# Attention probabilities turned and multiplied one step later, in a kernel of sixteen pipelined sequences

## The chip, the cores and the metric

The kernel runs on one core of a Trainium2 chip. The metric is device time in microseconds (us) from the first to the last instruction of one execution, with what lies around it. Five engines each work through a queue of their own in order: PE multiplies matrices, DVE, ACT and POOL work elementwise, SP issues DMAs. They meet only through semaphores, so an instruction that waits holds up all that stands behind it on its engine. PE writes to PSUM; DVE and ACT read PSUM, POOL doesn't.

## The reference

Sixteen sequences of 256 tokens and 128 features go through two layers. The first is a small two-layer network whose weights are trained while it runs: for each of its steps it computes an output with weights that the gradient of that step has just updated, so each step needs the one before it.

```
grads = grad(loss)(params, z, y)
new_params = params - LR * grads
out = recon(new_params, x @ t_q.T)        # scan over steps
```

The second is attention with 16 heads of 64 over 4 groups of keys and values, causal, with a window of 128 tokens and a learned sink in each head's denominator, and then a mixture of 32 experts of which each token uses 4.

```
q, k, v = split(rmsnorm(x) @ qkv_w + qkv_b);  q, k = rope(q), rope(k)
logits = where(mask, -inf, q k^T / 8)
attn = exp(logits - logaddexp(logsumexp(logits), sink))
x = x + (attn @ v) @ proj_w + proj_b
x = x + sum over the top 4 experts of gate * (silu(h2 Wg) * (h2 Wu)) @ Wd
```

## The kernel before, in words

The program has a short preparation, a part `layers` (from the start to about 940 us of the profile) and a part `experts`. The change is in `layers`, which is one loop of iterations n = 0 to 19. Iteration n holds five sequences at once, each at another stage: sequence n in the trained network (call it F), n-1 in the output with the new weights and its normalisation (O), n-2 in the projection to queries, keys and values and their rotation (N), n-3 in attention (A), n-4 in the output projection, the choice of experts and their slots (B). POOL sends the rows of sequence n-5 to the experts' table by indirect DMAs (line 94).

Each iteration has six steps, u = 0 to 5. Attention of a sequence is cut into six units of two head groups (h = 0, 1); units 0, 1, 3, 4 have two head pairs and queries 128 to 255, which see two blocks of keys; units 2 and 5 have four pairs and queries 0 to 127, one block. The order of the work within a step is written out for each engine in its function `iteration`, with tables `side` that place the stages of the other sequences; there is no planner. In step u of the kernel before:

- PE: projection of chunk u (line 555), scores of unit u+1 (lines 373, 379), probabilities times values of unit u-1 (line 408), stages of other sequences, turning of unit u's probabilities for h = 0 (line 393), more stages, turning of the rotated queries or keys (line 566), turning of unit u for h = 1.
- DVE: `quotients` for h = 0 of unit u (adds the sink term, line 672, reciprocal, 674, scales the probabilities in place, 678 or 682), the rotation's products (826 to 830), stages, `maxima` of unit u+1 (694 to 700), `quotients` for h = 1, stages.
- ACT: the sink's exponential (1008), exponentials of unit u for h = 0 (1020), copy of the turned probabilities of unit u-1 for h = 1 out of PSUM (1030), exponentials for h = 1, stages, copy of the product y of unit u-1 (1039), copy of the turned probabilities of unit u for h = 0, stages, copy of the turned queries or keys (`qk_out`).
- POOL: sum of the rotation's products (1152), then two sends of rows, then small stages: `rms2` in step 2, `norms` (1160 to 1174) in step 4, `spread` in step 5.

There is one buffer `prob` for each h: the exponentials of the next unit wait until this unit's has been turned. There are three banks of scores for two heads, so scores of unit u+1 wait until the exponentials of unit u, h = 0, have read theirs (line 370). The values `vv` have two buffers.

The chain through the trained weights runs over a whole iteration: `x_turn` (421) and `z_products` in step 0, `a_products` and `z_rows` in step 1, `gelus` on ACT (1063, another function table than Exp) and `residual_cols` (468, 470) in step 2, `residual_rows` (479 to 482), DVE's `slope_cdf` (759 to 765) and `hidden_grad` in step 3, `output` (PE 505, DVE 781 to 787) in step 4, and in step 5 `gradients` (517 to 523), DVE's `update` of the weights (803 to 808) and `norm_turn` (537). `norm_turn` waits for `update` and for `normed_rows` (795), which waits for POOL's `norms`, which wait for `output`. After `norm_turn` ACT's `hT_out` (1082) gives the next iteration's chunk 0 its input.

Of the kernel before, what the change touches and what calls it, by code (L numbers as in the profile page):

```python
# [24 lines left out]
P = 128  # L25
# [201 lines left out]
def layers(m):  # L227
# [12 lines left out]
    with ExitStack() as ctx:  # L240
# [27 lines left out]
        vv = sb("vv", [P, 2, TPS, KV * DH])  # L268
# [3 lines left out]
        sums, rec = (sb(n, [P, 2, 4]) for n in "sums rec".split())  # L272
        prob, probT = sb("prob", [P, 2, 512]), sb("probT", [P, 2, 512])
# [30 lines left out]
        def run(iteration):  # L304

            for n in range(SEQS + 4):
                iteration(n, n % 2)
# [45 lines left out]
        def _(pe):  # L353
# [29 lines left out]
            def turn_probs(n, par, u, h):  # L383
                A, ap, u, done = at_unit(n, par, u)
                if not live(A):
                    return
                if h == 0:
                    after(pe, s["probT"], 2 * done - 3)
                else:
                    after(pe, s["yT"], done - 1)  # L390
                pe.wait_ge(s["normed"], 2 * done - 1 + h)
                for k in range(4):
                    ins = tr(turned[h][:, k * P:(k + 1) * P], prob[:, h, k * P:(k + 1) * P], ident[:])  # L393
                ins.then_inc(s["t_ps"], 1)

            def values(n, par, u):
# [6 lines left out]
                for i in range(len(pairs)):  # L403
                    for k in range(2 if second else 1):
                        for h in range(2):
                            g = 2 * g2 + h
                            blk = 2 * i + k if second else i
                            ins = mm(turned[1][h * DH:(h + 1) * DH, i * P:(i + 1) * P], vv[:, ap, k, g * DH:(g + 1) * DH],  # L408
# [148 lines left out]

            def qk_turn(n, par, c):
# [11 lines left out]
            def project(t, k):  # L570

                def stage(n, par):
                    B = n - 4
                    if not live(B):
                        return
                    cols = slice(t * P, (t + 1) * P)
                    if t == 1 and k == 0:
                        after(pe, s["place"], B)

                    pe.wait_ge(s["yT"], B * UNITS + (2 if t else 3) + 3 * k)  # L580
                    if k == 0:
                        bias(side_g[:, cols], QKV, QKV + D)
                    for p in range(4 * k, 4 * k + 4):
                        ins = mm(side_g[:, cols], yT[:, par, p, cols], m["wproj"][:, p, :], start=False,
                                 stop=(p == PAIRS - 1))
                    ins.then_inc(s["proj_ps"], 1)
                return stage
# [21 lines left out]
            def ranks(n, par):  # L609
# [5 lines left out]
                for t in range(TPS):  # L615
# [6 lines left out]

            side = {0: [x_turn, project(1, 0)], 1: [z_products, project(1, 1)], 2: [a_products, project(0, 0)],
                    3: [z_rows, project(0, 1)], 5: [residual_cols], 6: [residual_rows, h2_turn],
                    7: [hidden_grad, gate], 8: [output], 10: [ranks, gradients], 11: [norm_turn]}

# [4 lines left out]

            def iteration(n, par):
                for u in range(UNITS):
                    if n != 2 or u == 0:
                        qkv(n, par, u)
                    if n == 2 and u < UNITS - 1:
                        qkv(n, par, u + 1)
# [5 lines left out]
                    if n < 3 or n == SEQS + 3:  # L643
                        keep_clock(1, turned[0] if n < 3 else score[2])
                    for stage in side.get(2 * u + 1, []):
                        stage(n, par)
                    qk_turn(n, par, u)
                    turn_probs(n, par, u, 1)
                    if n < 3 or n == SEQS + 3:
                        keep_clock(1, turned[0] if n < 3 else score[2])  # L650
# [6 lines left out]
            run(iteration)  # L657

        @block.vector
        def _(v):  # L660
            V = nc.vector

            def quotients(n, par, u, h):
# [5 lines left out]
                one = 2 * done - 1 + h  # L669
                v.wait_ge(s["es_out"], done)  # L670
                v.wait_ge(s["exped"], one)
                V.tensor_tensor(sums[:, h, 0:w], sums[:, h, 0:w], es[:, b, h, 0:w], ALU.add).then_inc(s["den"], 1)  # L672
                v.wait_ge(s["den"], one)
                V.reciprocal(rec[:, h, 0:w], sums[:, h, 0:w]).then_inc(s["rec"], 1)
                v.wait_ge(s["rec"], one)
                if second:
                    for j in range(w):
                        ins = V.tensor_scalar(prob[:, h, j * TOK:(j + 1) * TOK], prob[:, h, j * TOK:(j + 1) * TOK],  # L678
                                              rec[:, h, j:j + 1], None, ALU.mult)
                else:  # L680
                    rows = prob[:, h, :].rearrange("p (j k) -> p j k", j=w)
                    ins = V.tensor_tensor(rows, rows, rec[:, h, :][:, :, None].broadcast_to([P, w, P]), ALU.mult)
                ins.then_inc(s["normed"], 1)

            def maxima(n, par, u):
# [5 lines left out]
                sink = sink_s[:, pairs[0] // 2] if second else sink_f[:, pairs[0] // 4]  # L691
                v.wait_ge(s["s_ps"], done)
                for h in range(2):
                    V.tensor_reduce(mx[:, b, h, 0:w], score[(2 * u + h) % 3][:].rearrange("p (j k) -> p j k", j=w), AX.X,  # L694
                                    ALU.max).then_inc(s["mx"], 1)
                v.wait_ge(s["mx"], 2 * done)
                V.scalar_tensor_tensor(out=nm[:, b, :, 0:w], in0=mx[:, b, :, 0:w], scalar=-0.125, in1=sink,
                                       op0=ALU.mult, op1=ALU.min).then_inc(s["nm"], 1)
                v.wait_ge(s["nm"], done)
# [3 lines left out]
            def x_norm(n, par):  # L703

                F = n + 1
                if not live(F):
                    return
                if n in (0, 1):
                    v.wait_ge(s["rs0"], 2 * n + 4)
# [200 lines left out]
            def slots(n, par):  # L910
                B = n - 4
                if not live(B):
# [10 lines left out]
            side = {2: [a_bias], 3: [a_rows], 4: [attended], 5: [slope_pdf, h2_rows], 6: [slope_cdf],  # L923
                    7: [pick, hidden_grad], 8: [one_hot], 9: [output], 10: [normed_rows, places],
                    11: [x_norm, slots]}

            def first_stats(u):

# [7 lines left out]
            def iteration(n, par):  # L936
                for u in range(UNITS):
                    quotients(n, par, u, 0)
                    rope(n, par, u)
                    if n == 0:  # L940
                        first_stats(2 * u)
                    for stage in side.get(2 * u, []):
                        stage(n, par)
                    maxima(n, par, u + 1)
                    if u == 5:
                        update(n, par)
                    quotients(n, par, u, 1)
                    if u == 1:
                        centred(n, par)
                    if n == 0:  # L950
                        first_stats(2 * u + 1)
                    for stage in side.get(2 * u + 1, []):
                        stage(n, par)
# [40 lines left out]
            v.wait_ge(s["rs0"], 2)  # L994
            x_norm(-1, 1)
            run(iteration)

        @block.scalar
        def _(act):
# [10 lines left out]
            def exps(n, par, u, h):  # L1010
# [5 lines left out]
                after(act, s["t_ps"], 2 * done - 3 + h)  # L1016
# [610 lines left out]
```

## Time and profile before

| | us |
|---|---|
| three runs of the kernel | 1217.37, 1218.06, 1222.43 |
| their median | 1218.06 |
| the profiled execution's own time | 1224.69 |
| its span, first to last instruction | 1222.9 |
| granted PE clock, mean of the span, of full speed | 0.891 |

The profiled execution is a single one. Its span lies 1.8 us below its own time, and its time 6.6 us above the median of the runs. In the profile an engine's row says what it did and when; the time in brackets is idle time just before an instruction, with the work that released it. Several instructions of one line are merged into one row with their count. Full speed of PE's clock is 2.4 GHz; a granted clock of 0.50 is 1.2 GHz.

### The profile page before, as it was taken

The numbers are of one execution on the slowest core, as the hardware profiler recorded it, in microseconds if no ns is written. First come the engines' busy times: TensorE is split into PE (matmuls) and PEld (weight loads), VectorE is DVE, ScalarE is ACT, GpSimd is POOL, SyncE is SP. The second block draws the span as 40 slices with busy tenths as digits, with TensorE's granted clock in tenths as the row PEclk, the third lists the DMA queues.
The fourth block names the chain that finished last, engine by engine and source line by source line (L and its number), as shares of the span: only waits on it lengthen the run. The fifth ranks groups of instructions, "written<-read, shape, count | busy, mean of one in ns | idle before, by whom it ended". The sixth has DMA issues, their size and how long they took to land. (4 is left out here: it accounts for less than half of the span.)

```text
span 1222.9 us, 21965 instructions
## 1 busy us (share of the span) xinstructions
PE 951.9 (78%) x6783; PEld 702.7 (57%) x6865; DVE 778.4 (64%) x2648; ACT 608.3 (50%) x1987; POOL 495.6 (41%) x643
## 2 busy tenths in 40 slices
PE   4778888897989888898988988888877399777710
PEld 2445666565666666575666666555555288666610
DVE  4455687778677776868786777877764344333307
ACT  1017565655646565655756555665654155444400
POOL 2221223334334333334343333434432457777760
PEclk7788999899889899998989989998997599999855
DMA  5999999990000000000000000000000144443119
GB/s 142 267 356 376 374 376 371 370 300 10 16 6 18 9 15 11 11 10 11 15 8 18 6 15 11 11 15 11 15 15 15 55 115 134 132 115 104 52 54 338
DMA packets 98372, 131.54 MB, mean 108 GB/s; under 512 B 15025, under 2 KB 54866, under 8 KB 98258
## 3 DMA queue, kind: packets, MB, share of 16 engines
q1 hardware_dynamic: 84690, 108.36, 26.9%
q0 software_dynamic: 9216, 19.68, 4.6%
q10 hardware_dynamic: 4352, 2.10, 0.6%
q8 instruction: 57, 0.93, 0.3%
q14 instruction: 57, 0.47, 0.1%
HBM read 30.34 MB, written 99.75 MB: 106 GB/s over the span
## 5 line engine op out<-in xcount | busy, mean ns | idle before, releaser
L1152 POOL TENSOR_TENSOR l_t_cos<-l_t_cos,l_t_sin 128x512 f32<-128x512 f32 (+1 forms) x96 | 104.4, 1088 | 434.1 <-DVE l_t_sin L830 434.1
L1020 ACT ACTIVATE l_prob<-l_score,l_nm 128x128 f32<-128x128 f32 (+1 forms) x512 | 210.8, 431 | 0.0
L393 PE MATMUL l_turned<-ident_sb,l_prob 128*128 128x128 f32 x768 | 127.3, 291 | 90.2 <-DVE l_prob L678 52.4
L1345 POOL DMA_INDIRECT expert_out<-e_yo,e_dest x160 | 153.7, 960 | 69.1 <-issue 37.2
L1030 ACT COPY l_probT<-l_turned 128x512 f32<-128x512 f32 x192 | 113.0, 589 | 102.5 <-PE l_turned L393 101.5
L393 PEld LDWEIGHTS l_turned<-ident_sb,l_prob 128*128 128x128 f32 x768 | 91.4, 149 | 108.2 <-issue 107.3
L94 POOL DMA_INDIRECT expert_rows<-h,slot x128 | 128.9, 1007 | 37.6 <-issue 32.4
L694 DVE TENSOR_REDUCE l_mx<-l_score 128x2 f32<-128x512 f32 (+1 forms) x192 | 122.7, 680 | 10.6 <-PE l_score L379 10.2
L555 PE MATMUL l_side_q<-wqkv_sb,l_hT 128*128 128x512 f32 x186 | 118.5, 725 | 12.0 <-issue 4.1
L379 PE MATMUL l_score<-l_kT,l_qT 64*128 64x128 f32 (+1 forms) x1024 | 115.4, 356 | 0.0
L1020 ACT ACTIVATION_READ_ACCUMULATOR l_prob<-l_score,l_nm 128x1 f32 x512 | 110.7, 216 | 0.0
L379 PEld LDWEIGHTS l_score<-l_kT,l_qT 64*128 64x128 f32 x1024 | 79.0, 195 | 52.5 <-issue 48.9
L408 PE MATMUL l_turned<-l_probT,l_vv 128*64 128x128 f32 x1536 | 106.9, 282 | 1.4 <-ACT l_probT L1030 1.4
L408 PEld LDWEIGHTS l_turned<-l_probT,l_vv 128*64 128x64 f32 x1536 | 83.4, 138 | 27.4 <-issue 21.5
L1486 ACT ACTIVATE e_yo<-e_p_y,e_mine 128x128 f32<-128x128 f32 x160 | 45.8, 369 | 88.3 <-DMA expert_out<-e_yo,e_dest 77.3
L1039 ACT COPY l_yT<-l_turned 128x256 f32<-128x256 f32 (+1 forms) x96 | 42.2, 439 | 88.8 <-PE l_turned L408 88.8
L672 DVE TENSOR_TENSOR l_sums<-l_sums,l_es 128x2 f32<-128x2 f32 (+1 forms) x192 | 30.6, 159 | 86.1 <-ACT l_prob L1020 85.5
L678 DVE TENSOR_SCALAR l_prob<-l_prob,l_rec 128x256 f32<-128x256 f32 x256 | 79.8, 354 | 4.5
L1427 DVE COPY e_hidT<-e_p_h 128x512 f32<-128x512 f32 x40 | 27.7, 692 | 83.9 <-PE e_p_h L1553 78.0
L1543 PE MATMUL e_p_up<-wup_sb,e_xT 128*128 x320 | 79.7, 394 | 0.0
L1562 PE MATMUL e_p_y<-wdown_sb,e_hidT 128*128 x320 | 48.0, 297 | 29.6 <-ACT e_yo L1486 29.5
L826 DVE TENSOR_TENSOR l_t_cos<-l_side_q,rope_sb 128x512 f32<-128x512 f32 (+1 forms) x93 | 55.4, 596 | 24.4 <-PE l_side_q L555 24.1
(234 smaller groups left out, 1937.2 us busy)
## 6 DMA issues: line engine op xcount, KB each, us to landing
expert_rows<-zeros SPq DMA_DIRECT2D x32, 2240.0 KB, 21.9
e_xt<-expert_rows SPq DMA_DIRECT2D x160, 70.0 KB
e_rows<-expert_out SPq DMA_DIRECT2D x16, 512.0 KB, 5.9
wup_sb<-in_wup SPq DMA_DIRECT2D x1, 4096.0 KB, 14.5
expert_out<-e_yo,e_dest POOLq DMA_INDIRECT x160
expert_rows<-zeros SPq DMA_DIRECT2D x32, 70.0 KB, 2.1
expert_rows<-zeros SPq DMA_DIRECT2D x4, 560.0 KB, 12.9
expert_rows<-h,slot POOLq DMA_INDIRECT x128, 2.3
```

Source lines behind the costliest of these rows:

```text
L94: m["nc"].gpsimd.indirect_dma_start(m["xs"], bass.IndirectOffsetOnAxis(ap=m["slot"][:, par, c:c + 1], axis=0), m["h2"][:, par, c // TOPK, ...
L379: ins = mm(bank[h][:, i * w:(i + 1) * w], qT[rows, ap, p, tok], kT[rows, ap, g2, 0:w], start=False, stop=(i == len(pairs) - 1))
L393: ins = tr(turned[h][:, k * P:(k + 1) * P], prob[:, h, k * P:(k + 1) * P], ident[:])
L408: ins = mm(turned[1][h * DH:(h + 1) * DH, i * P:(i + 1) * P], vv[:, ap, k, g * DH:(g + 1) * DH], probT[:, h, blk * P:(blk + 1) * P], start ...
L555: mm(dst[:], hT[:, t * P:(t + 1) * P], m["wqkv"][:, part * 512:(part + 1) * 512], start=False, stop=True).then_inc(s["qkv_ps"], 1)
L678: ins = V.tensor_scalar(prob[:, h, j * TOK:(j + 1) * TOK], prob[:, h, j * TOK:(j + 1) * TOK], rec[:, h, j:j + 1], None, ALU.mult)
L694: V.tensor_reduce(mx[:, b, h, 0:w], score[(2 * u + h) % 3][:].rearrange("p (j k) -> p j k", j=w), AX.X, ALU.max).then_inc(s["mx"], 1)
L1020: ins = A_.activation(prob[:, h, cols], score[(2 * u + h) % 3][:, cols], ACT.Exp, bias=nm[:, b, h, j:j + 1], scale=0.125, accum_out=sums[: ...
L1030: A_.copy(probT[:, h, :], turned[h][:]).then_inc(s["probT"], 1)
L1152: g.tensor_tensor(t_cos[:, c % 2, 0:w], t_cos[:, c % 2, 0:w], t_sin[:, c % 2, 0:w], ALU.add).then_inc(s["added"], 1)
L1345: g_.indirect_dma_start(m["ys"], bass.IndirectOffsetOnAxis(ap=dest[:, g % FOUND, j:j + 1], axis=0), yo[:, g % YO, j, :], None).then_inc(se ...
L1543: ins = mm(p_up[g % 2][:, j, :], xT[:, g % 2, j, :], m["wup"][:, bass.ds(expert(g, j) * (2 * DFF), 2 * DFF)], start=True, stop=True)
```

## The change

Turning, copying and multiplying of unit u's probabilities move from step u (and the first part of step u+1) to step u+1. On PE the product with the values now ends the step, and the two turnings stand behind the scores. On ACT both heads' exponentials open the step, then come the sink's exponential, the copies of the turned probabilities of the unit before, and the copy of y ends the step. On DVE the sums and reciprocals of both heads of a unit are one operation each, placed behind the maxima of the next unit and interleaved with its shift and sink terms, and both scalings follow. `prob`, `sums` and `rec` get a second buffer by u % 2, `vv` a third. The loops over steps and the tables `side` are written out as lists of calls; DVE runs one iteration (n = -1) ahead for the first `x_norm`, and ACT and PE one iteration beyond, in which nothing is live. POOL's order and its DMAs are the same calls as before.

```diff
-        vv = sb("vv", [P, 2, TPS, KV * DH])
+        vv = sb("vv", [P, 3, TPS, KV * DH])
...
-        sums, rec = (sb(n, [P, 2, 4]) for n in "sums rec".split())
-        prob, probT = sb("prob", [P, 2, 512]), sb("probT", [P, 2, 512])
+        sums, rec = (sb(n, [P, 2, 2, 4]) for n in "sums rec".split())
+        prob, probT = sb("prob", [P, 2, 2, 512]), sb("probT", [P, 2, 512])
...
             def iteration(n, par):
-                for u in range(UNITS):
...
-                    scores(n, par, u + 1)
-                    values(n, par, u - 1)
-                    for stage in side.get(2 * u, []):
-                        stage(n, par)
-                    turn_probs(n, par, u, 0)
...
-                    qk_turn(n, par, u)
-                    turn_probs(n, par, u, 1)
...
+                chunk(n, par, 2)
+                scores(n, par, 3)
+                turn_probs(n, par, 1, 0)
+                turn_probs(n, par, 1, 1)
+                idle(n, par, 4)
+                residual_cols(n, par)
+                qk_turn(n, par, 2)
+                values(n, par, 1)
...
+                chunk(n, par, 5)
+                scores(n + 1, 1 - par, 0)
+                turn_probs(n, par, 4, 0)
+                ranks(n, par)
+                gradients(n, par)
+                turn_probs(n, par, 4, 1)
+                idle(n, par, 10)
+                norm_turn(n, par)
+                qk_turn(n, par, 5)
+                values(n, par, 4)
...
         @block.vector
...
-            def quotients(n, par, u, h):
+            def sums_out(n, par, u):
...
+                v.wait_ge(s["es_out"], done)
+                v.wait_ge(s["exped"], 2 * done)
+                V.tensor_tensor(sums[:, b, :, 0:w], sums[:, b, :, 0:w], es[:, b, :, 0:w], ALU.add).then_inc(s["den"], 1)
...
+                V.reciprocal(rec[:, b, :, 0:w], sums[:, b, :, 0:w]).then_inc(s["rec"], 1)
...
+                slope_cdf(n, par)
+                maxima(n, par, 4)
+                shifts(n, par, 4)
+                sums_out(n, par, 3)
+                sinks(n, par, 4)
+                recips(n, par, 3)
+                scaled(n, par, 3, 0)
+                scaled(n, par, 3, 1)
...
+                pick(n, par)
+                hidden_grad(n, par)
+                rope(n, par, 4)
...
+                scaled(n, par, 4, 1)
...
+                output(n, par)
+                rope(n, par, 5)
...
+                normed_rows(n, par)
+                places(n, par)
+                maxima(n + 1, 1 - par, 0)
+                shifts(n + 1, 1 - par, 0)
+                sums_out(n, par, 5)
+                sinks(n + 1, 1 - par, 0)
+                recips(n, par, 5)
+                update(n, par)
+                scaled(n, par, 5, 0)
...
         @block.scalar
...
-                after(act, s["t_ps"], 2 * done - 3 + h)
+                after(act, s["t_ps"], 2 * done - 5 + h)
...
-                    sink_terms(n, par, u)
-                    exps(n, par, u, 0)
-                    take_probs(n, par, u - 1, 1)
-                    exps(n, par, u, 1)
...
-                    take_y(n, par, u - 1)
-                    take_probs(n, par, u, 0)
...
-                    qk_out(n, par, u)
...
+                exps(n, par, 2, 0)
+                exps(n, par, 2, 1)
+                sink_terms(n, par, 2)
+                take_probs(n, par, 1, 0)
+                gelus(n, par)
+                take_probs(n, par, 1, 1)
+                rT_out(n, par)
+                qk_out(n, par, 2)
+                take_y(n, par, 1)
+                exps(n, par, 3, 0)
```

The lists of the other steps follow the same pattern; `chunk` is the projection with the exception for n = 2, `idle` the matmuls that fill PE in iterations 0 to 2 and 19.

## Rows read from the trace of the kernel before

**Rows 1.** Stretches (us, from:to, length): busy PE, PEld, DVE, ACT, POOL; clock; DMA.

```profile
142.70:798.00 655.30, 565.21 (x4319) 411.24 (x4379) 494.76 (x1688) 385.04 (x1307) 241.13 (x340) 0.93 0.23 81
...
581.30:634.10 52.80, 45.76 (x362) 33.34 (x366) 41.31 (x142) 31.94 (x110) 20.43 (x29) 0.97 0.04 12
...
848.90:899.20 50.30, 39.98 (x301) 26.53 (x304) 34.44 (x114) 27.71 (x101) 17.85 (x20) 0.90 0.04 13
...
899.20:938.40 39.20, 30.44 (x273) 23.00 (x274) 25.51 (x95) 23.54 (x89) 12.12 (x15) 0.87 0.05 18
```

**Rows 2.** Line 393 (probabilities turned): what PE waited for, us, times.

```profile
  DVE l_prob L678: 53.2, 44
  DVE l_prob L682: 37.8, 26
```

**Rows 3.** PE in order of time: start, us, instruction, idle before it and its releaser.

```profile
580.75 0.44 PE L537 MATMUL l_side_f<-ident_sb,l_hn 128*128 128x128 f32 x2
...
582.61 1.02 PE L555 MATMUL l_side_q<-wqkv_sb,l_hT 128*128 128x512 f32 x2
...
599.38 1.02 PE L555 MATMUL l_side_q<-wqkv_sb,l_hT 128*128 128x512 f32 x2
...
600.52 0.59 PE L373 MATMUL l_score<-mask,ident_bf 128*128 128x512 bf16 x2
...
602.11 1.09 PE L408 MATMUL l_turned<-l_probT,l_vv 128*64 128x128 f32 x16
...
607.37 0.63 PE L393 MATMUL l_turned<-ident_sb,l_prob 128*128 128x128 f32 x4 [1.98 <-DVE l_prob L682]
...
608.91 0.59 PE L373 MATMUL l_score<-mask,ident_bf 128*128 128x512 bf16 x2
...
616.62 0.63 PE L393 MATMUL l_turned<-ident_sb,l_prob 128*128 128x128 f32 x4 [1.40 <-DVE l_prob L678]
...
633.56 0.44 PE L537 MATMUL l_side_f<-ident_sb,l_hn 128*128 128x128 f32 x2 [1.15 <-DVE b_sb L808]
```

**Rows 4.** DVE and POOL in order of time, same iteration.

```profile
612.93 0.23 DVE L759 COPY l_h<-l_side_f 128x66 f32<-128x66 f32 x1 [1.57 <-PE l_side_f L482]
...
619.28 0.69 DVE L826 TENSOR_TENSOR l_t_cos<-l_side_q,rope_sb 128x512 f32<-128x512 f32 x1 [0.79 <-PE l_side_q L555]
...
626.44 0.25 DVE L787 BATCH_NORM_AGGREGATE l_mv<-l_stats 128x2 f32<-128x6 f32 x2
...
629.81 1.52 DVE L795 TENSOR_SCALAR l_hn<-x_all,l_mv,l_rms 128x128 f32<-128x128 f32 x2 [0.70 <-POOL l_rms L1174]
...
629.58 0.20 POOL L1174 TENSOR_TENSOR l_rms<-l_sq,l_rs 128x2 f32<-128x2 f32 x1
```

**Rows 5.** ACT in order of time, same iteration.

```profile
594.23 0.37 ACT L1039 COPY l_yT<-l_turned 128x256 f32<-128x256 f32 x1 [0.63 <-PE l_turned L408]
...
598.88 0.36 ACT L1020 ACTIVATE l_prob<-l_score,l_nm 128x128 f32<-128x128 f32 x1
...
602.28 1.28 ACT L1063 ACT_TABLE_LOAD   x1
...
603.58 0.63 ACT L1063 ACTIVATE l_hT<-l_aT 32x512 f32<-32x512 f32 x1
...
606.03 1.28 ACT L1008 ACT_TABLE_LOAD   x1
...
607.44 0.46 ACT L1020 ACTIVATE l_prob<-l_score,l_nm 128x256 f32<-128x256 f32 x1
```

**Rows 6.** DVE by line and shape: one or two heads' sums: busy us, mean ns.

```profile
L672 DVE TENSOR_TENSOR l_sums<-l_sums,l_es 128x2 f32<-128x2 f32 x128 | 20.1, 157 | 74.0 <-ACT l_prob L1020 73.4 <-ACT l_es L1008 0.3 <-issue 0.3
...
L672 DVE TENSOR_TENSOR l_sums<-l_sums,l_es 128x4 f32<-128x4 f32 x64 | 10.4, 163 | 12.1 <-ACT l_prob L1020 12.0
```

**Rows 7.** One-us stretches, columns as in rows 1.

```profile
607.20:608.20 1.00, 0.83 (x6) 0.82 (x7) 0.97 (x7) 0.99 (x5) 0.92 (x3) 1.00 0.20 72
618.20:619.20 1.00, 1.00 (x3) 0.28 (x2) 0.29 (x2) 1.00 (x8) 0.00 (x0) 0.50 0.02 8
```

More of the change, by code:

```diff
@@ L302, in live, with run @@
             return 0 <= k < SEQS
-        def run(iteration):
-            for n in range(SEQS + 4):
+        def run(iteration, early=0, late=0):
+            for n in range(-early, SEQS + 4 + late):
                 iteration(n, n % 2)
@@ L567, in qk_turn, with project @@
                 ins.then_inc(s["qk_ps"], 1)
[L570 to L587, printed above, removed]
+            def project(n, par, t, k):
+                B = n - 4
+                if not live(B):
+                    return
+                cols = slice(t * P, (t + 1) * P)
+                if t == 1 and k == 0:
+                    after(pe, s["place"], B)
+                pe.wait_ge(s["yT"], B * UNITS + (2 if t else 3) + 3 * k)
+                if k == 0:
+                    bias(side_g[:, cols], QKV, QKV + D)
+                for p in range(4 * k, 4 * k + 4):
+                    ins = mm(side_g[:, cols], yT[:, par, p, cols], m["wproj"][:, p, :], start=False,
+                             stop=(p == PAIRS - 1))
+                ins.then_inc(s["proj_ps"], 1)
             def h2_turn(n, par):
@@ L695, in maxima, with shifts @@
                                     ALU.max).then_inc(s["mx"], 1)
+            def shifts(n, par, u):
+                A, ap, u, done = at_unit(n, par, u)
+                if not live(A):
+                    return
+                pairs, second = unit(u)
+                b, w = u % 2, len(pairs)
+                sink = sink_s[:, pairs[0] // 2] if second else sink_f[:, pairs[0] // 4]
                 v.wait_ge(s["mx"], 2 * done)
@@ L698, in maxima, with sinks @@
                                        op0=ALU.mult, op1=ALU.min).then_inc(s["nm"], 1)
+            def sinks(n, par, u):
+                A, ap, u, done = at_unit(n, par, u)
+                if not live(A):
+                    return
+                pairs, second = unit(u)
+                b, w = u % 2, len(pairs)
+                sink = sink_s[:, pairs[0] // 2] if second else sink_f[:, pairs[0] // 4]
                 v.wait_ge(s["nm"], done)
@@ L921, in slots, with first_stats @@
                 V.tensor_copy(slot[:, par].rearrange("p (t k) -> p t k", t=TPS), slotf).then_inc(s["slot"], 1)
[L923 to L927, printed above, removed]
+            def first_stats(n, par, u):
+                if n != 0:
+                    return
                 if u == 3:
@@ L936, in iteration @@
             def iteration(n, par):
[L937 to L953, printed above, removed]
+                rope(n, par, 0)
```

257 lines of the change are left out of this document (200 added, 57 removed).

## The prediction

> **What bounds the kernel now.** I read the stretches first [rows 1]. Twelve whole iterations (n = 4 to 15) fill 142.7 to 798.0: 655.3 / 12 = 54.6 us each. One of them, from 581.3, took 52.8 at a mean clock of 0.97, against 0.93 over all twelve. In it PE was busy 45.8 us, DVE 41.3, ACT 31.9. No engine fills it, so waits between engines set its length. Next come the waits on line 393 [rows 2]: PE stood 53.2 + 37.8 = 91.0 us for DVE's scaled probabilities, 5.7 us in each of the sixteen sequences. This is the wait that the change is about. Two of these stand in the iteration from 581.3: 1.98 us in step 2, 1.40 in step 3 [rows 3].
>
> Whether removing it helps depends on what else ends at the same time, so I cut that iteration in order of time [rows 3 to 5] at events of the chain through the trained weights:
> - a, from the projection of chunk 0 to that of chunk 2, 582.61 to 599.38: 16.77;
> - b, to DVE's start of `slope_cdf` at 612.93: 13.55;
> - c, to the end of `output`'s statistics, 626.44 + 0.25: 13.76;
> - d, to `norm_turn` at 633.56: 6.87;
> - e, to the next chunk 0: 1.86, from the pair an iteration earlier (580.75 to 582.61), as PE was at half clock at the later one.
>
> The sum is 52.8. a is PE's work. In b PE and ACT hand to each other. c is DVE at work almost without a pause: its one pause that stands in the rows is 0.79 us at 619.28 [rows 4], for a projection at half clock (granted 1.00 at 607 us, 0.50 at 618 [rows 7], that is 2.4 and 1.2 GHz). In d POOL's `norms` end at 629.78, then DVE does `normed_rows`, the next maxima and `update`; PE waits 1.15 us for it [rows 3, 4]. So c and d, 20.6 us, go by DVE and POOL, and PE's waits there hide behind them.
>
> **The change, part by part.** *Fewer operations on DVE.* Six sums and six reciprocals fall away per iteration. The sum over both heads is as wide as one that already runs: 163 ns for four columns, 157 for two [rows 6], so joining costs nothing; I take 0.4 us per unit for the pair that goes. In a and b DVE waits for others, so it gives nothing there. In c, three head-wise blocks are replaced by two joint ones with all four scalings ahead of `output`: one pair of 0.4 goes, one scaling of about 0.5 comes in, and the interleaving saves 0.2 twice. c falls from 13.76 to 12.7, of which 0.79 is the pause at half clock. In d the joint sum and reciprocal now stand before `update`: 6.87 becomes 6.95. The joint sum waits for both heads' exponentials, and behind it in DVE's queue stand the reciprocal, the scalings and `update`; since the exponentials now open ACT's step and the sum comes after the next maxima, I cost that wait at nothing; if ACT were late, `update` would be late with it.
>
> *Buffers and POOL.* The second `prob`, the third `vv` and the extra iterations issue nothing new. POOL's calls, its indirect DMAs and SP's queue keep their order, so no queue is passed.
>
> *ACT's order, in a.* The copy of y now ends ACT's step, behind PE's product that ends PE's step, and the next exponentials stand behind it. The copy takes 0.37 and starts 0.1 after the product [rows 5]. From the first exponential of a four-pair unit to the scores it releases are 600.52 - 598.88 = 1.64 us [rows 3, 5]; I estimate 1.1 for a two-pair unit with half as many instructions. PE covers 1.1 by the chunk's projection. Left are 0.4 to 0.9 us of wait before each scores. Of line 393's 5.7 us per sequence I put 0.5 into steps 0 and 1, by what steps 2 and 3 leave. a becomes 17.2; its bounds are 16.3 (copy fully hidden) and 18.
>
> *ACT's order, in b.* Before, the first exponential of unit 2 began at 598.88, 0.50 before chunk 2's projection; now it begins 0.15 after it: scores come 0.65 later. Before, the load of the gelu table began 602.28 - 598.88 = 3.40 after that exponential; now it stands behind the copy of turned probabilities, which needs the scores (602.11 - 600.52 = 1.59) and the turning (0.63); the copy is as wide as gelu (0.63), of which some 0.5 before the next may start: 1.64 + 1.59 + 1.2 = 4.4. Before, the load back to Exp began 606.03 - 603.58 = 2.45 after gelu; now the product (1.09 [rows 3], 1.03 to the next start) and the copy of y (0.37) come first, while some 0.8 of ACT's copies fall beside them: 3.05, an estimate. Together 0.65 + 1.0 + 0.6 = 2.25: the exponentials of unit 3 begin that much later than 607.44, and the scores they release start at 607.44 + 2.25 + 1.1 = 610.8 instead of 608.91. Before, PE's wait of 1.98 covered this table load; that cover goes. Behind these scores a turning stands instead of the product, 0.5 less. b becomes 13.55 + 1.9 - 0.5 = 14.9; bounds 13.5 and 15.5, and I take the value near the upper one because each term is a row's duration on an engine that works in order.
>
> A table load takes 1.28 us and the activation behind it starts 0.02 later [rows 5]. The Trainium skill ("ScalarE: Activation LUTs", What ACT_TABLE_LOAD costs) puts a switch at 2.66 us, with a drain of 1380 ns behind the load; by it the two loads of b would add 2.8 us and the forecast would be 33 us higher. The rows show no such drain, and the sum goes by them.
>
> *e.* PE's product with the values (1.03) replaces the last turning with its wait: 1.97. The five make 17.2 + 14.9 + 12.7 + 6.95 + 1.97 = 53.7, against 52.8 - 0.79 = 52.0 for before at full clock. What is late next is `update`: PE should wait about 3 us for it at `norm_turn`.
>
> *The clock.* The twelve iterations average 54.6, so half clock costs 2.6 us each; at 0.93 against 0.97 there are about two such stretches an iteration, 0.8 (the pause at 619.28) to 1.3 each. They began after waits of PE, but not after all: not after 1.98, but after 1.40 [rows 3, 7]. The new waits, 2 us for gelu and before scores of unit 4, 3 at `norm_turn`, are as many and lie where PE's work is on the path. I take 2.2, with bounds 0 and 4: 55.9 an iteration, +1.3, times twelve: +15.6 us.
>
> *The other iterations.* n = 3 and 16 lack parts of c or d: I estimate -1.5 each. From 848.9 to 899.2 (n = 17) there is no trained chain: 50.3 us with PE busy 40.0 at a clock of 0.90 [rows 1], some 36 at full clock. There the removed waits were not covered: 36 + 6 x 0.9 + 1 for the clock = 42.5, a gain of 7.5. From 899.2 to 938.4 no projection covers the copy of y and the exponentials: 0.4 a step, +2.4. Sum: -8.1. The experts have no edit.
>
> **Sum.** +15.6 - 8.1 = +7.5. The profiled execution took 1224.7 of its own (span 1222.9 and 1.8 around it), so it would take 1232; its time is 6.6 above the median, 1218.06, so I expect 1226.
>
> **The rivals.**
> 1. *The forecast*: the exposed exponentials take the place of the removed wait, and the last iterations give part back. 1226 (1210 to 1238). Chance 0.43.
> 2. *ACT's new order is hidden* (the copy of y and the loads fit into PE's stages): a 16.3, b 13.55, the rest as above, 51.5 + 2.2 = 53.7, -0.9 times twelve, -8: 1199. For it: in a and b lies most of DVE's time without work (52.8 - 41.3 = 11.5), so it is not late there. Against: the copy needs the product, which is the last on PE's list. 0.20.
> 3. *The whole wait is won*: 1218 - 91 = 1127. It needs c and d to overlap with other steps, but their order in DVE's queue is as before. 0.04.
> 4. *The clock*, the rival with loss: a third stretch at half clock per iteration, begun by the wait at `norm_turn` and falling on e and a, PE's work. 53.7 + 3 x 1.3 = 57.6, +3.0 times twelve, -8: 1246. It decides if the clock falls at that wait each time. 0.23. The Trainium skill ("TensorE: Matmul & The Clock Gate", HAM oscillation) says that an engine which waits between bursts restarts each at half clock; the rows agree in part, after 1.40 but not after 1.98.
> 5. *No change in the iterations*: the longer b meets a shorter clock loss, 54.6 stays, only the last iterations gain: 1210. 0.10.
>
> **The numbers.** A measurement of this kernel can tell about 0.5%, 6 us. Faster than 1212: rival 2 but a trace of it, 3, half of 5 and a tail of the forecast: 0.33. Within: 0.20. Slower than 1224: most of the forecast and rival 4: 0.47. The range leaves out rival 3, the better third of 2 and the worse third of 4: 1188 to 1260; the forecast's own range stands above.
>
> **What would show it.** In the profile after: PE's waits for scaled probabilities at line 393 near zero; new waits of PE before scores (line 373), released by the exponentials, longest in step 3; b near 14.9, c near 12.7; about 3 us before `norm_turn`; the stretch of n = 17 under 44. If b stays at 13.5, or the wait at `norm_turn` vanishes, the steps on ACT's order are wrong; if the mean clock over the twelve leaves 0.90 to 0.96, the clock's term is.

## The result, and the profile after the change

The change makes the kernel slower, by 1.4%. Four runs of it took 1233.59 to 1238.90 us, median 1236.11; four of the kernel before, beside them, 1217.37 to 1222.43, median 1219.35 (the three of the table above and a fourth). The ratio is 1.0136 with a 95% interval of 1.0099 to 1.0173. The profiled execution has a span of 1231.8 us against 1222.9.

The first view is that of stretches, as in [rows 1]: the twelve whole iterations, one of them, and n = 17.

```profile
140.30:811.30 671.00, 565.71 (x4380) 404.65 (x4378) 460.58 (x1547) 393.65 (x1309) 238.00 (x340) 0.95 0.23 81
530.80:586.30 55.50, 46.45 (x367) 33.46 (x366) 38.48 (x130) 32.79 (x110) 20.52 (x29) 0.96 0.04 12
861.80:905.20 43.40, 37.61 (x305) 24.91 (x303) 32.60 (x105) 28.22 (x107) 17.88 (x20) 0.97 0.05 15
```

Twelve iterations take 671.0 us, 55.9 each (from `hT_out` to `hT_out`, as it was 656.0 before; the window of [rows 1] begins 0.7 later). PE is busy as long as before (565.7 and 565.2) and DVE 34 us less, so it is waiting that has grown. What PE waited for in these iterations (us in total, times, longest), first before, then after:

```profile
PE l_turned L393 <- DVE l_prob L678: 40.5, 36, 2.0
PE l_turned L393 <- DVE l_prob L682: 25.8, 19, 2.3
PE l_side_f L537 <- DVE b_sb L808: 11.8, 8, 1.6
```

```profile
PE l_score L373 <- ACT l_prob L1152: 47.1, 64, 1.6
PE l_side_f L537 <- DVE b_sb L886: 33.3, 12, 3.1
PE l_side_f L470 <- ACT l_hT L1195: 20.9, 12, 1.7
```

The wait at line 393, which was the point of the change, is gone (66.3 us before). 47.1 before the scores, 20.9 for gelu and 21.5 more at `norm_turn` (33.3 against 11.8) have come in its place. One iteration in order of time, PE first (start, us, instruction, idle before it), as in [rows 3]:

```profile
529.98 0.69 PE L537 MATMUL l_side_f<-ident_sb,l_hn 128*128 128x128 f32 x2 [2.70 <-DVE b_sb L886]
...
533.54 1.02 PE L555 MATMUL l_side_q<-wqkv_sb,l_hT 128*128 128x512 f32 x2
...
550.86 1.02 PE L555 MATMUL l_side_q<-wqkv_sb,l_hT 128*128 128x512 f32 x2
552.67 0.59 PE L373 MATMUL l_score<-mask,ident_bf 128*128 128x512 bf16 x2 [0.79 <-ACT l_prob L1152]
...
557.53 0.70 PE L470 MATMUL l_side_f<-l_hT,fast 128*128 128x256 f32 x2 [1.75 <-ACT l_hT L1195]
...
562.50 0.60 PE L373 MATMUL l_score<-mask,ident_bf 128*128 128x512 bf16 x2 [1.63 <-ACT l_prob L1152]
...
585.49 0.69 PE L537 MATMUL l_side_f<-ident_sb,l_hn 128*128 128x128 f32 x2 [2.68 <-DVE b_sb L886]
```

ACT in the same iteration shows what the scores and gelu stood behind: the copy of y (line 1171) ahead of the exponentials of units 2 and 3, and the copy of turned probabilities (1162) ahead of gelu. Gelu and unit 3 also need a load of a function table, which begins only when that copy is done:

```profile
550.75 0.37 ACT L1171 COPY l_yT<-l_turned 128x256 f32<-128x256 f32 x1 [0.66 <-PE l_turned L408]
551.01 0.37 ACT L1152 ACTIVATE l_prob<-l_score,l_nm 128x128 f32<-128x128 f32 x1
...
554.95 0.59 ACT L1162 COPY l_probT<-l_turned 128x512 f32<-128x512 f32 x1 [0.93 <-PE l_turned L393]
555.55 1.28 ACT L1195 ACT_TABLE_LOAD   x1
556.85 0.63 ACT L1195 ACTIVATE l_hT<-l_aT 32x512 f32<-32x512 f32 x1
...
559.74 0.37 ACT L1171 COPY l_yT<-l_turned 128x256 f32<-128x256 f32 x1 [0.45 <-PE l_turned L408]
560.13 1.28 ACT L1152 ACT_TABLE_LOAD   x1
561.42 0.47 ACT L1152 ACTIVATE l_prob<-l_score,l_nm 128x256 f32<-128x256 f32 x1
```

And DVE ([rows 4] show it before): `update` stands behind the next maxima and the joint sum, and PE waits for it at 585.49.

```profile
565.91 0.23 DVE L837 COPY l_h<-l_side_f 128x66 f32<-128x66 f32 x1 [3.65 <-PE l_side_f L482]
...
578.30 0.25 DVE L865 BATCH_NORM_AGGREGATE l_mv<-l_stats 128x2 f32<-128x6 f32 x2
...
581.66 1.52 DVE L873 TENSOR_SCALAR l_hn<-x_all,l_mv,l_rms 128x128 f32<-128x128 f32 x2 [1.88 <-POOL l_rms L1341]
...
583.31 1.26 DVE L756 TENSOR_REDUCE l_mx<-l_score 128x2 f32<-128x512 f32 x2
...
584.68 0.17 DVE L722 TENSOR_TENSOR l_sums<-l_sums,l_es 128x8 f32<-128x8 f32 x1
...
585.00 0.17 DVE L881 SCALAR_TENSOR_TENSOR fast<-l_side_f,fast 128x64 f32<-128x64 f32 x1
```

Cut at the prediction's events and averaged over n = 4 to 15, here for all kernels of this study (us; "from n = 17" runs from chunk 0 of n = 17 to the experts' first product). The stretches are those of the one profiled execution, the medians those of all runs:

| kernel | a | b | c | d | e | sum | from n = 17 | median |
|---|---|---|---|---|---|---|---|---|
| before | 17.05 | 14.12 | 13.97 | 7.28 | 2.25 | 54.7 | 106.4 | 1219.35 |
| after | 17.49 | 15.22 | 12.70 | 6.98 | 3.63 | 56.0 | 102.7 | 1236.11 |
| exps_first | 16.82 | 13.44 | 12.69 | 6.98 | 3.65 | 53.6 | 87.7 | 1185.58 |
| fill_wait | 17.32 | 15.17 | 12.70 | 6.98 | 2.06 | 54.2 | 101.8 | 1214.95 |
| norm_last | 17.05 | 15.11 | 12.70 | 6.98 | 1.29 | 53.1 | 102.7 | 1196.90 |
| update_early | 17.31 | 15.06 | 12.70 | 5.09 | 2.40 | 52.6 | 103.4 | 1189.62 |
| split_sums | 17.60 | 15.28 | 12.94 | 7.08 | 3.70 | 56.6 | 102.7 | 1244.63 |
| gelus_first | 17.57 | 13.56 | 12.69 | 6.96 | 3.66 | 54.5 | 99.6 | 1209.50 |
| combo1 | 16.47 | 13.44 | 12.69 | 5.09 | 1.62 | 49.3 | 87.8 | 1127.45 |
| combo2 | 16.46 | 11.96 | 12.69 | 5.09 | 1.71 | 47.9 | 87.3 | 1108.13 |
| combo3 | 16.47 | 11.98 | 11.49 | 5.28 | 1.62 | 46.8 | 87.4 | 1094.64 |
| before_update | 17.36 | 15.21 | 13.87 | 5.81 | 3.57 | 55.8 | 106.4 | 1241.28 |

The clock moved with the waits. Before, PE ran at half clock for a part of c in ten of the twelve iterations; in the two others c took 12.9. Over the twelve PE was at half clock for 85 us, 35 of them in c and 15 in e. Two of before's stretches c, the second of them at full clock, and two pieces around `norm_turn` after the change (columns as above, the granted clock third from the end):

```profile
612.90:626.70 13.80, 10.93 (x81) 7.86 (x82) 12.31 (x46) 8.11 (x31) 3.26 (x3) 0.88 0.03 12
668.90:681.70 12.80, 9.21 (x81) 7.25 (x82) 12.14 (x47) 8.44 (x31) 2.22 (x2) 1.00 0.04 12
```

```profile
582.70:584.50 1.80, 0.11 (x2) 0.00 (x0) 1.80 (x6) 0.59 (x1) 1.17 (x4) 0.97 0.00 0
585.50:586.50 1.00, 1.00 (x5) 1.00 (x6) 1.00 (x2) 0.22 (x1) 0.00 (x0) 0.50 0.03 8
```

After the change c runs at full clock, and the half clock falls behind the wait at `norm_turn` in all twelve iterations, on e, and in seven of them it reaches into the next a. There the product with the values took 1.93 us at 531.46, and 1.09 at full clock elsewhere. PE is at half clock for 68 us of the twelve, 41 of them in e. Ten more lie in b: in n = 7, 10 and 12 the clock falls soon after the wait for gelu as well, which is the same 1.75 us in all twelve. In n = 7 the next projection takes 1.91 where it takes 1.02 at full clock:

```profile
333.70 0.70 PE L470 MATMUL l_side_f<-l_hT,fast 128*128 128x256 f32 x2 [1.75 <-ACT l_hT L1195]
...
336.68 1.91 PE L555 MATMUL l_side_q<-wqkv_sb,l_hT 128*128 128x512 f32 x2
```

### The profile page after: what moved, and what is told of

It reads as the page before. It is cut to its first block and busy times, and to the rows that moved or that the text cites. A ratio compares the mean times of both kernels' runs of the same rounds, so it can differ in the third digit from the quotient of the medians.

```text
span 1231.8 us, 21755 instructions
## 1 busy us (share of the span) xinstructions
PE 947.3 (77%) x6865; PEld 691.4 (56%) x6865; DVE 730.5 (59%) x2456; ACT 615.9 (50%) x1987; POOL 491.1 (40%) x643
## 5 line engine op out<-in xcount | busy, mean ns | idle before, releaser
L408 PE MATMUL l_turned<-l_probT,l_vv 128*64 128x128 f32 x1536 | 118.4, 302 | 11.9 <-ACT l_probT L1162 11.9
L393 PE MATMUL l_turned<-ident_sb,l_prob 128*128 128x128 f32 x768 | 119.1, 282 | 0.0
L379 PE MATMUL l_score<-l_kT,l_qT 64*128 64x128 f32 (+1 forms) x1024 | 111.1, 346 | 0.0
L408 PEld LDWEIGHTS l_turned<-l_probT,l_vv 128*64 128x64 f32 x1536 | 92.8, 150 | 31.1 <-ACT l_probT L1162 16.8
L373 PE MATMUL l_score<-mask,ident_bf 128*128 128x512 bf16 x192 | 59.6, 393 | 64.8 <-ACT l_prob L1152 64.7
L555 PE MATMUL l_side_q<-wqkv_sb,l_hT 128*128 128x512 f32 x186 | 105.4, 651 | 0.0
L379 PEld LDWEIGHTS l_score<-l_kT,l_qT 64*128 64x128 f32 x1024 | 76.0, 188 | 45.5 <-issue 42.5
L393 PEld LDWEIGHTS l_turned<-ident_sb,l_prob 128*128 128x128 f32 x768 | 85.9, 143 | 25.3 <-issue 21.4
L373 PEld LDWEIGHTS l_score<-mask,ident_bf 128*128 128x128 bf16 x192 | 12.3, 98 | 144.8 <-ACT l_prob L1152 90.0
L741 DVE TENSOR_SCALAR l_prob<-l_prob,l_rec 128x256 f32<-128x256 f32 x256 | 74.8, 355 | 2.3
```

Of the source, the lines that this page charges most:

```text
L379: ins = mm(bank[h][:, i * w:(i + 1) * w], qT[rows, ap, p, tok], kT[rows, ap, g2, 0:w], start=False, stop=(i == len(pairs) - 1))
L393: ins = tr(turned[h][:, k * P:(k + 1) * P], prob[:, u % 2, h, k * P:(k + 1) * P], ident[:])
L555: mm(dst[:], hT[:, t * P:(t + 1) * P], m["wqkv"][:, part * 512:(part + 1) * 512], start=False, stop=True).then_inc(s["qkv_ps"], 1)
L741: ins = V.tensor_scalar(prob[:, b, h, j * TOK:(j + 1) * TOK], prob[:, b, h, j * TOK:(j + 1) * TOK], rec[:, b, h, j:j + 1], None, ALU.mult)
```

## The experiments

All ratios are against the kernel before, run beside each; its medians there were 1219.34 to 1221.64, so times of different rounds compare to about 2 us. The edits are made in the changed kernel unless said otherwise.

**exps_first: the next exponentials ahead of the copy of y.** ACT's list, here step 1; the other five are alike.

```diff
                 qk_out(n, par, 1)
-                take_y(n, par, 0)
                 exps(n, par, 2, 0)
+                take_y(n, par, 0)
                 exps(n, par, 2, 1)
```

> The changed kernel with one edit on ACT: the exponentials of the next unit for the first head group stand ahead of the copy of y, not behind it. Theory (ACT's new order put the exponentials behind the copy of y, and PE's scores wait for them, 47.1 us in the twelve whole iterations): the waits on line 373 fall by more than half; stretch a goes from 17.5 to about 16.8, b from 15.2 to about 13.8 (scores of steps 2 and 3 each 0.8 earlier), c, d and e stay; twelve times 2.1 is 25, so about 1211 us against 1236. Rival (the scores only wait for what other engines hold up anyway): a and b stay within 0.3 each and the time within 5 us of the changed kernel's 1236.

1185.58 us, ratio 0.9689 (0.9643 to 0.9736): 50 below the changed kernel, twice what was expected. The rival falls. PE's waits in the twelve iterations:

```profile
PE l_side_f L537 <- DVE b_sb L886: 39.5, 12, 3.6
PE l_side_f L470 <- ACT l_hT L1195: 21.0, 12, 1.7
PE l_score L373 <- ACT l_prob L1152: 17.8, 21, 1.1
```

The waits before scores fell from 47.1 to 17.8, a by 0.67, b by 1.78. That is 12 x 2.43 = 29 (all five stretches together), near the 25 expected. What was not expected is the end: from n = 17 on, where no trained chain covers ACT, another 15.0 are gained (PE's waits before scores fall there from 10.7 to 1.7), and 4.8 in the iterations n = 3 and 16 (45.9 and 47.5 us from `hT_out` to `hT_out`, against 49.2 and 49.0).

**fill_wait: PE kept busy ahead of norm_turn.**

```diff
+            def fill_wait(n, par):
...
+                    pe.wait_ge(s["exped"], 2 * done)
+                    keep_clock(10, score[2])
...
                 idle(n, par, 10)
+                fill_wait(n, par)
                 norm_turn(n, par)
```

> The changed kernel with ten matrix products of no use (512 columns each, into a free bank of scores) put into PE's wait ahead of the last turning of the iteration (norm_turn). Theory (PE's clock falls to half because PE waits 2.7 us there, and stretch e behind it is PE's work): the granted clock stays at 1.00 there, e goes from 3.63 to about 2.0, the other stretches stay; twelve times 1.6 is 20, so about 1217 us. Rival 1 (the fall has another cause): e stays at 3.6 and the time at 1236. Rival 2 (the fall only moves on to the wait for gelu in b or to the scores in a): e at 2.0, but a or b 1 to 1.5 longer, and the time within 8 us of 1236.

1214.95 us, ratio 0.9929 (0.9908 to 0.9949), so 21 below the changed kernel with 2.3 us more work on PE. One iteration's end:

```profile
517.78 2.32 PE L629 MATMUL l_score<-l_filler,ones_bf 128*128 128x512 bf16 x10
520.64 0.44 PE L537 MATMUL l_side_f<-ident_sb,l_hn 128*128 128x128 f32 x2 [0.54 <-DVE b_sb L893]
...
521.44 1.09 PE L408 MATMUL l_turned<-l_probT,l_vv 128*64 128x128 f32 x16
```

e is 2.06 in all twelve iterations, the mean clock 0.99. So the wait starts the half clock there, and what it cost in e is 3.63 - 2.06 = 1.57 us, 19 over the twelve; rival 1 falls. The half clock did not move on, so rival 2 falls too: a and b are a little shorter, and it still falls in b in two iterations, where it was three.

**norm_last: the wait filled with the step's own work.**

```diff
-                norm_turn(n, par)
                 qk_turn(n, par, 5)
                 values(n, par, 4)
+                norm_turn(n, par)
...
-                hT_out(n, par)
                 qk_out(n, par, 5)
                 take_y(n, par, 4)
+                hT_out(n, par)
```

> The changed kernel with the turning of rotated queries of chunk 5 and the product with the values of unit 4 ahead of norm_turn on PE, so that they fall into its wait, and hT_out behind the copy of y on ACT. Theory (in e the product and the turning stand between norm_turn and chunk 0 for nothing): e goes from 3.63 to about 1.4, d stays at 6.95 because norm_turn waits for update as before; twelve times 2.2 is 26, about 1210 us. Rival (the half clock goes with the wait, which is still 1 us long, and falls on a instead): e at 1.4 to 1.8 but a longer by 1 to 1.5, about 1225 us.

1196.90 us, ratio 0.9776 (0.9729 to 0.9824): 39 lower, where 26 were expected. e is 1.29 and d unchanged. PE still waits 0.9 us at `norm_turn` in most iterations, and the clock fell on a behind it in one of the twelve only, so the rival falls. a is shorter as well, 16.92 in most iterations: the exponentials of unit 0 now begin at 514.28, ahead of chunk 0's projection, and PE's wait of 0.22 for them is gone.

```profile
511.36 1.09 PE L408 MATMUL l_turned<-l_probT,l_vv 128*64 128x128 f32 x16
513.37 0.44 PE L537 MATMUL l_side_f<-ident_sb,l_hn 128*128 128x128 f32 x2 [0.92 <-DVE b_sb L886]
514.44 0.39 PE L357 MATMUL l_side_q<-bias_bf,ones_bf 128*128 128x512 bf16 x1 [0.63 <-ACT l_hT L1214]
514.66 1.02 PE L555 MATMUL l_side_q<-wqkv_sb,l_hT 128*128 128x512 f32 x2
```

**update_early: the weights' update ahead of the next unit's operations on DVE.**

```diff
                 normed_rows(n, par)
+                update(n, par)
                 places(n, par)
                 maxima(n + 1, 1 - par, 0)
...
                 recips(n, par, 5)
-                update(n, par)
```

> The changed kernel with DVE's update of the weights right behind normed_rows, ahead of the maxima, shift, joint sum, sink term and joint reciprocal of the next unit. Theory (norm_turn waits for update, and update for these five operations): d goes from 6.95 to about 5.1; PE's wait there shrinks from 2.7 to 0.9 us, and if that is too short for the clock to fall e goes to 2.0 too: twelve times 1.85 is 22 (about 1214 us), with the clock twelve times 3.4 is 41 (about 1195 us). Rival (the next maxima, 0.5 us later now, and with them the exponentials and scores of the next iteration are as much on the path): d at 5.1 but e and a longer together by 1 to 2, and the time within 10 us of 1236.

1189.62 us, ratio 0.9715 (0.9666 to 0.9763): 46 lower, d 5.09, e 2.40, and a no longer, so the rival falls. The theory holds, with the clock in most iterations: in nine iterations e is 2.05 or 2.06, in three 3.15 to 3.62. The wait was 0.83 in an iteration of either kind, so its length does not decide alone; the product with the values behind it shows the clock:

```profile
504.66 0.44 PE L537 MATMUL l_side_f<-ident_sb,l_hn 128*128 128x128 f32 x2 [0.83 <-DVE b_sb L886]
...
505.46 1.09 PE L408 MATMUL l_turned<-l_probT,l_vv 128*64 128x128 f32 x16
...
608.97 0.64 PE L537 MATMUL l_side_f<-ident_sb,l_hn 128*128 128x128 f32 x2 [0.83 <-DVE b_sb L886]
...
610.39 1.97 PE L408 MATMUL l_turned<-l_probT,l_vv 128*64 128x128 f32 x16
```

**before_update: the same edit in the kernel before.** This asks whether the changed order of the turnings matters for it.

```diff
-                    7: [pick, hidden_grad], 8: [one_hot], 9: [output], 10: [normed_rows, places],
+                    7: [pick, hidden_grad], 8: [one_hot], 9: [output], 10: [normed_rows, update, places],
...
-                    if u == 5:
-                        update(n, par)
```

> The kernel before with one edit on DVE: update right behind normed_rows, ahead of the next maxima (the edit that took 46 us off the changed kernel). Theory (before the change, the last turning of the iteration stands between norm_turn and chunk 0 and waits for probabilities that DVE scales behind those maxima, so that the wait on line 393 takes over what update gives): d goes from 7.28 to about 5.4, e from 2.25 to about 4.0, and the time stays within 6 us of the kernel before, about 1220. Rival (the two kernels share this chain, and the edit is worth in both what it takes from d): d 5.4, e 2.25, twelve times 1.8 is 22, about 1198 us.

1241.28 us, ratio 1.0194 (1.0159 to 1.0228): slower than before, which neither the theory nor the rival had. d fell by 1.47 as in the theory, e rose by 1.32, because the last turning still waits for the scaling that stands behind the maxima:

```profile
584.52 0.44 PE L537 MATMUL l_side_f<-ident_sb,l_hn 128*128 128x128 f32 x2
584.79 0.60 PE L566 MATMUL l_side_q<-ident_sb,l_t_cos 128*128 128x128 f32 x4
587.40 0.63 PE L393 MATMUL l_turned<-ident_sb,l_prob 128*128 128x128 f32 x4 [2.01 <-DVE l_prob L682]
```

So nothing is won there, and b lost 1.1 besides. PE's clock now falls in b in all twelve iterations (before in four), behind the same wait of 1.97 us in step 2 that it had outlasted at full clock in [rows 3, 7]. Over the twelve it is low for 85 us in either kernel: before, 14 of them lay in b and 31 in d and e, now 41 in b and none in d and e. Why it now falls in b is open. The two profiled executions lie 12 us apart (1236.72 and 1224.69), the medians 22. The edit is worth 46 us with the change and less than nothing without it.

**split_sums: the joint operations undone.**

```diff
-                V.tensor_tensor(sums[:, b, :, 0:w], sums[:, b, :, 0:w], es[:, b, :, 0:w], ALU.add).then_inc(s["den"], 1)
+                for h in range(2):
+                    V.tensor_tensor(sums[:, b, h, 0:w], sums[:, b, h, 0:w], es[:, b, h, 0:w], ALU.add).then_inc(s["den"], 1)
...
-                V.reciprocal(rec[:, b, :, 0:w], sums[:, b, :, 0:w]).then_inc(s["rec"], 1)
+                for h in range(2):
+                    V.reciprocal(rec[:, b, h, 0:w], sums[:, b, h, 0:w]).then_inc(s["rec"], 1)
```

> The changed kernel with one part of the change undone: the sums and the reciprocals of the two heads are two operations each again, at the same places in DVE's list. Theory of the prediction (a pair that goes is worth 0.4 us where DVE ends last): c, with two units in it, 0.6 to 0.8 longer than 12.70, d 0.3 to 0.4 longer than 6.98, a, b and e as they are; twelve times 1.1 is 13, about 1249 us. Rival (the second operation follows the first without a pause, as in the row of before where the next starts some 0.1 us later, so that the pair is worth 0.2): c 0.4 longer, d 0.2, about 1243 us. If nothing changes, c and d of the changed kernel are shorter for another reason than the joint operations.

1244.63 us, ratio 1.0198 (1.0163 to 1.0234), 8.5 above the changed kernel. c is 0.24 longer with two units in it, d 0.10 with one: 0.1 per unit, half of the rival's price and a quarter of the theory's. The other 3 of the 7 us that the five stretches add up to lie in a, b and e. Two sums one behind the other take 0.23 us where one takes 0.16:

```profile
585.62 0.23 DVE L723 TENSOR_TENSOR l_sums<-l_sums,l_es 128x2 f32<-128x2 f32 x2
585.88 0.23 DVE L732 RECIPROCAL l_rec<-l_sums 128x2 f32<-128x2 f32 x2
```

**gelus_first: gelu's table load ahead of the copy.**

```diff
                 sink_terms(n, par, 2)
-                take_probs(n, par, 1, 0)
                 gelus(n, par)
+                take_probs(n, par, 1, 0)
                 take_probs(n, par, 1, 1)
```

> The changed kernel with gelu and its table load ahead of the copy of the turned probabilities of unit 1 on ACT (step 2), where they stood behind it. Theory (in b PE waits 1.75 us for gelu because its load stands behind that copy, which itself waits for the turning): the wait on line 470 falls from 1.75 us an iteration to 0.2 to 0.5, b goes from 15.2 to about 14.0, the rest stays; twelve times 1.2 is 14, about 1222 us. Rival (b is set by the load back to the exponential and the exponentials of unit 3, which then only stand as late as before): the wait on line 470 falls, the one before the scores of step 3 grows by as much, b within 0.3 of 15.2 and the time within 5 us of 1236.

1209.50 us, ratio 0.9910 (0.9877 to 0.9943), 27 lower, where 14 were expected. b fell by 1.66, from 15.05 to 13.55 where the clock was full, and the half clock behind the wait for gelu is gone from it; another 5 us lie in n = 3 and from n = 17 on. The wait for gelu is gone and the one before the scores of step 3 stayed at 1.63, so the rival falls: everything behind gelu came earlier together.

```profile
542.68 0.70 PE L470 MATMUL l_side_f<-l_hT,fast 128*128 128x256 f32 x2 [0.23 <-ACT l_hT L1195]
...
547.67 0.60 PE L373 MATMUL l_score<-mask,ident_bf 128*128 128x512 bf16 x2 [1.63 <-ACT l_prob L1152]
```

**The edits together.** combo1 has exps_first, update_early, and in step 5 the queries of chunk 5 turned ahead of `norm_turn` on PE and copied ahead of `hT_out` on ACT; combo2 also gelus_first; combo3 also `output` ahead of the scaling of unit 4.

```diff
+                qk_turn(n, par, 5)
                 norm_turn(n, par)
-                qk_turn(n, par, 5)
...
+                output(n, par)
                 scaled(n, par, 4, 0)
                 scaled(n, par, 4, 1)
                 first_stats(n, par, 9)
-                output(n, par)
```

> The changed kernel with three edits together: the exponentials of the next unit's first head group ahead of the copy of y on ACT, update right behind normed_rows on DVE, and the turning of chunk 5 ahead of norm_turn on PE with hT_out behind its copy on ACT. Theory (three separate places of the same iteration): their gains add up: a 16.3 to 16.8, b 13.3, c 12.7, d 5.1, e about 1.5; 49.0 to 49.5 an iteration against 56.0, twelve times 6.7 is 80, and 15 in the last iterations as in the kernel with the exponentials alone: about 1140 us. Rival (with the maxima behind update the exponentials of unit 0 are late, and the scores of step 0 wait for them): e or a longer by 0.5 to 1, about 1150 us.

> The three edits of combo1 and gelu ahead of the copy of the turned probabilities of unit 1. Theory: another 1.0 to 1.3 us in b, twelve times that and a little in the last iterations: 12 to 16 us below combo1. Rival (the exponentials of unit 3 set b): within 4 us of combo1.

> The edits of combo2 and, on DVE, output ahead of the scaling of unit 4's probabilities, which stood in front of it. Theory (c ends with DVE's list, and norms, normed_rows and update follow it): c goes from 12.69 to about 11.6, d stays near 5.1; twelve times 1.1 is 13, about 1095 us. Rival (in d the gradients on PE come last, which stand behind the scores of step 5 and their exponentials): d grows by what c loses, and the time stays within 4 us of combo2.

1127.45 us (ratio 0.9239, 0.9206 to 0.9271), 1108.13 (0.9077, 0.9045 to 0.9108) and 1094.64 (0.8985, 0.8969 to 0.9001): the theory's sums each time, somewhat exceeded by the first two (in combo1 n = 3 and 16, which the theory left out, are 8.7 us shorter together). The three rivals fall; of combo3's, 0.2 of the 1.2 that c lost came back in d. In combo3's twelve iterations (stretch and waits) the mean clock is 1.00 and PE is busy 533 of 562 us. Of the waits above only those before scores are left with some size, so these iterations are now for the most part PE's own work:

```profile
132.00:694.00 562.00, 533.06 (x4384) 389.57 (x4382) 457.12 (x1545) 382.82 (x1309) 239.64 (x339) 1.00 0.29 102
```

```profile
PE l_score L373 <- ACT l_prob L1152: 20.1, 24, 1.1
PE l_side_f L470 <- ACT l_hT L1195: 5.1, 12, 0.4
```

## Why the prediction was right, and where its terms were not

The mechanism and the range were right: exposed exponentials and table loads took the place of the removed wait. So was the sign, though a slower kernel had only a chance of 0.47; 1236 lies 10 above the forecast, near the upper end of its own range, 1210 to 1238.

- **a.** Forecast 17.2; 17.14 to 17.39 where no half clock reaches it, 17.49 on average. With the exponentials ahead of the copy a falls to 16.31 at best, the bound that the prediction gave for a copy fully hidden.
- **b.** Forecast 14.9; 15.05 in most iterations, 15.22 on average with the half clock of three. Its terms: gelu's load 4.4 after the first exponential of unit 2 (555.55 - 551.01 = 4.54), the load back 3.05 after gelu (560.13 - 556.85 = 3.28), the scores of step 3 at 11.4 after chunk 2 (562.50 - 550.86 = 11.64). Both table loads were followed by their function within 0.02 us. The price of the Trainium skill ("ScalarE: Activation LUTs", What ACT_TABLE_LOAD costs), a drain of 1380 ns more, shows in no row here either.
- **c.** Forecast 12.7 and measured 12.70, but partly by luck, with terms that only cancelled. The pair of joint operations, taken at 0.4 us, is worth 0.1, and what was to cost 0.1 on balance (one scaling more, less waiting) saved about as much. From 12.9 at full clock to 12.64 there is 0.25 for the edits together; the other us of the 1.27 that c lost is the half clock that left it (0.79 was taken for it).
- **d.** Forecast 6.95, measured 6.94 to 6.96 in most iterations, with the wait of about 3 us at `norm_turn` (2.7). `update` was what came late next, as said, and the joint sum waited for nothing (584.68, straight behind the shift and ahead of `update`).
- **e and the clock.** e at full clock was forecast at 1.97 (2.06 in fill_wait) and the clock at 2.2 per iteration. Most iterations of fill_wait, in which the clock did not fall, took 54.0, so after the change it costs about 2.0. Where it falls was only half seen: 1.57 of it lies on e, behind `norm_turn`. That is the place of the fourth rival; but no third stretch was added, since the one in c went, and the mean clock rose from 0.93 to 0.95.
- **The other iterations.** Cut from chunk 0 to chunk 0, the twelve took 16.1 more (143.32 to 799.35 before, 141.39 to 813.54 after; forecast 15.6), n = 3 1.2 less and n = 16 1.4 less (50.06 to 48.85 and 49.72 to 48.28; forecast 1.5 each), n = 17 6.9 less (50.3 to 43.4; forecast 7.5), n = 18 and the way to the experts 3.2 more (106.4 - 50.3 = 56.1 to 102.7 - 43.4 = 59.3; forecast 2.4). With 0.7 less ahead of n = 3, which the forecast left out, and 0.2 less behind these it is the +8.9 of the profile.
- **From the sum to the median.** The sum gave +7.5 and 1232 for a profiled execution; the profiled one took 1233.59, +8.9. The step that failed is the last: the offset of 6.6 between before's profiled execution and its median was carried over. After the change the profiled execution is the fastest of its four runs, so the medians lie 16.8 apart and not 8. This offset was scatter of single executions and should have widened the range, not moved its middle.

Of the rivals, the fifth (no change in the iterations) falls with the 1.3 us that each of them gained in length. The second (ACT's order is hidden, 1199) is not what the change does; exps_first shows what it would have been worth, 1186. The third, the whole wait won (1127), the change alone never came near; combo2 and combo3 go below it, but by removing other waits, on ACT and at `norm_turn`.

## What to carry to other kernels

When an operation is moved one step later, the wait is not gone until it is known what stands behind the moved operation's last part on every engine that works in order; here it was the copy of y on ACT, and turning two neighbours round in each step gave back three times what the change had lost. A change can lose time and still be the condition for winning more: `update` ahead of the maxima cost 22 us before it, in part by the clock for a reason that is open, and brought 46 after it. And an iteration cut at events of its chain, each stretch costed from rows of its own, predicted the whole within 0.1 us per iteration. That close it was by luck: the stretches at full clock were 0.3 short, and the term without a row of its own, the clock, was 0.2 too large and half wrong in place.

## What the runs showed of the hardware that was not expected

- The granted clock falls from 1.00 to 0.50 after some of PE's waits and not after others of the same length: after 2.7 to 3.1 us at `norm_turn` in twelve of twelve iterations of the changed kernel, after the 1.75 for gelu in three of them and not in nine, after 0.83 in one iteration and not in another of update_early. The Trainium skill ("TensorE: Matmul & The Clock Gate", HAM oscillation) tells of a kernel whose bursts of work, with waits between them that are longer than most here, each start at the low clock. The trace agrees for the longest waits, at `norm_turn`, and shows that shorter ones can do it too; no single length tells the cases apart here.
- Products of no use, put into one wait, made a kernel 21 us faster, 1.7%, with nothing else changed; the same wait filled with the step's own work brought 39.
